# Mixture-of-experts results: scaled at the copy from PSUM and added in memory by the scatter, instead of scattered apart and summed on VectorE

## The reference, cut to what matters

```python
scores = sigmoid(x @ gate_w)                      # 32 experts
...                                               # 2 of 4 groups are masked out, the best 6 of the rest are taken
weights = take_along_axis(original_scores, selected_experts, axis=-1)
weights = weights / sum(weights, axis=-1, keepdims=True)
xs = repeat(x, 6, axis=0)[sort_idx]               # sorted by expert
d = ragged_dot(silu(xs @ w_gate) * (xs @ w_up), w_down, group_sizes)
expert_out = sum(d[unsort_idx].reshape(T, 6, H) * weights[..., None], axis=1)
shared = silu(x @ sw_gate) * (x @ sw_up) @ sw_down
return expert_out + shared
```

## Time and profile before

| | us |
|---|---|
| median of 3 runs | 1883.34 (1881.84 to 1884.39) |
| the profiled execution, its own time | 1883.7 |
| its span | 1881.9 |
| TensorE busy in the span | 1711.4 (91%) |
| VectorE / ScalarE / GpSimd busy | 1413.4 / 1098.0 / 1099.5 |
| `experts`, from its first instruction to its last add | 1296.7 to 1627.6 |

### The profile page before, as it was taken

The page is one execution under the profiler, slowest core; times in us unless marked ns, Lnnn a source line. Parts: engine busy times, 40 slices in busy tenths (PEclk is TensorE's granted clock), DMA queues, the critical chain, the costliest instruction groups (busy, mean ns, idle before and its releaser), DMA issues. The chain is left out here.

```text
span 1881.9 us, 41627 instructions
## 1 busy us (share of the span) xinstructions
PE 1711.4 (91%) x14679; PEld 1308.2 (70%) x14679; DVE 1413.4 (75%) x3752; ACT 1098.0 (58%) x2774; POOL 1099.5 (58%) x1718
## 2 busy tenths in 40 slices
PE   4899999999999999999999999978999997189988
PEld 3678787878777788877877887755555554139974
DVE  7898786888977878878788788766567764775746
ACT  6577776667777667767666676643133332174534
POOL 5578595686776957868668578410366663181210
PEclk9899999999999999999999999997999999596998
DMA  3210111011010000100000000436299895400100
GB/s 124 74 51 30 60 35 53 19 36 46 18 38 31 24 19 18 63 26 19 20 31 23 24 1 24 140 109 227 71 279 269 272 268 173 144 19 23 45 7 26
DMA packets 74649, 140.24 MB, mean 75 GB/s; under 512 B 10921, under 2 KB 44818, under 8 KB 74194
## 3 DMA queue, kind: packets, MB, share of 16 engines
q1 hardware_dynamic: 63634, 105.37, 18.3%
q0 software_dynamic: 9984, 30.42, 4.8%
q10 hardware_dynamic: 832, 1.84, 0.3%
HBM read 111.73 MB, written 25.86 MB: 73 GB/s over the span
## 5 line engine op out<-in xcount | busy, mean ns | idle before, releaser
L920 DVE TENSOR_TENSOR att_pT<-att_pT 128x512 bf16<-128x512 f32 (+1 forms) x512 | 321.1, 651 | 175.6 <-ACT att_pT L729 173.0
L565 PE MATMUL att_out<-att_V,att_pT 128*128 128x128 bf16 x5760 | 388.2, 220 | 13.6 <-DVE att_pT L920 11.8
L565 PEld LDWEIGHTS att_out<-att_V,att_pT 128*128 128x128 bf16 x5760 | 350.3, 98 | 40.5 <-DVE att_pT L920 24.0
L729 ACT ACTIVATE att_pT<-att_pT 128x512 bf16<-128x512 f32 (+1 forms) x512 | 277.9, 571 | 131.9 <-PE att_pT L551 131.9
L735 ACT ACTIVATE att_prob<-att_scores,att_negmax 128x512 f32<-128x512 f32 (+1 forms) x512 | 330.2, 654 | 19.5 <-DVE att_negmax L909 19.5
L542 PE MATMUL att_scores<-att_K,att_Q 128*128 128x512 bf16 (+1 forms) x1536 | 324.9, 361 | 0.1
L907 DVE TENSOR_REDUCE att_mx<-att_scores 128x1 f32<-128x512 f32 (+1 forms) x512 | 291.4, 631 | 1.3 <-PE att_scores L542 1.2
L551 PE MATMUL att_pT<-att_ident,att_prob 128*128 128x128 f32 x1920 | 275.9, 275 | 0.0
L542 PEld LDWEIGHTS att_scores<-att_K,att_Q 128*128 128x128 bf16 x1536 | 151.1, 98 | 145.1 <-issue 3.5
L551 PEld LDWEIGHTS att_pT<-att_ident,att_prob 128*128 128x128 f32 x1920 | 210.1, 141 | 0.9
L465 PE MATMUL att_aux<-att_wkv,att_kvT 128*128 128x256 bf16 x1350 | 168.2, 274 | 22.7 <-DVE att_aT L881 14.8
(11 more groups left out here) (342 smaller groups left out, 3230.2 us busy)
## 6 DMA issues: line engine op xcount, KB each, us to landing
moe_wa<-in_wa_l SPq DMA_DIRECT2D x80, 480.0 KB
att_wq<-wq_s SPq DMA_DIRECT2D x12, 512.0 KB, 3.7
att_wo<-wo_s SPq DMA_DIRECT2D x12, 512.0 KB, 3.8
moe_y<-y_s SPq DMA_DIRECT2D x8, 768.0 KB, 4.5
att_stage<-in_ctx_l SPq DMA_DIRECT2D x9, 512.0 KB, 4.2
near_s<-att_windows POOLq DMA_DIRECT2D x8, 576.0 KB, 5.6
win_near<-near_s SPq DMA_DIRECT2D x32, 144.0 KB
moe_wb<-in_wb_l SPq DMA_DIRECT2D x80, 48.0 KB
```

Source lines behind the costliest of these rows:

```text
L565: last = nc.tensor.matmul(out_ps[:, i % 2, :], pT[:, i % 2, a, k, :], V[:, par, k, w, :], start=(k, a, w) == (0, 0, 0), stop=(k, a) == (KT ...
L729: nc.scalar.activation(pT[:, i % 2, 0, 4 * j:4 * j + m, :], pT_ps[j % 2][:, 0:m, :], ACT.Copy).then_inc(s["pt_hi"], 1)
L920: nc.vector.tensor_tensor(pT[:, i % 2, 1, 4 * j:4 * j + m, :], pT_ps[j % 2][:, 0:m, :], pT[:, i % 2, 0, 4 * j:4 * j + m, :], ALU.subtract) ...
```

## The change

The share no longer meets its row on VectorE behind the scatter, but on ScalarE ahead of it:

- The table `xrow_s` has 32 more columns: each token's gates. SyncE writes them in a DMA at the block's start; the gathers fetch rows of 1152 bytes in place of 1024.
- VectorE makes once a one-hot table of each slot's expert (`tiles_experts`, 128x2560), and for each slot multiplies the gathered gates by it with a running sum (`slot_shares`): one share per lane. ScalarE's copy of the result takes it as its scale.
- The scatter adds to what lies in memory (`compute_op=ALU.add`), into `sum0_s` and `sum1_s` in turn, each with one row per token. A scatter waits until the one two slots before it has landed, as both may hold the same token. GpSimd fills `zeros`, SyncE writes it to both accumulators (1 MB and 128 KB each) ahead of the weight fetches.
- In the end 8 DMAs of 256 KB bring both accumulators back and VectorE adds them with 8 instructions of 128x512. `y6`, `add_row`, `shares` and the turn half of the table are gone.

```diff
+                sp.dma_start(t["xrow_s"][0:TOK, D:XROW].rearrange("(n p) e -> p n e", p=P), gates[:, :, :]).then_inc(s["gates_out"], 16)
                 sp.wait_ge(s["const_in"], 16)
                 sp.dma_start(t["xrow_s"][EMPTY:EMPTY + 1, :], const[0:1, CONST["zero"]]).then_inc(s["zero_out"], 16)
+                sp.wait_ge(s["zeros_set"], 1)
+                for a in range(SUMS):
+                    sp.dma_start(t[f"sum{a}_s"][0:TOK, :].rearrange("(n p) d -> p n d", p=P), zeros[:, :, :]).then_inc(s["sums_zero"], 16)
+                    sp.dma_start(t[f"sum{a}_s"][TOK:TOK + P, :], zeros[:, 0, :]).then_inc(s["sums_zero"], 16)
...
-                for n in range(TT):
-                    wait(sp, s["added"], SHARED + TOPK * (n - 1) if n > 1 else 0)
-                    rows = t["y_s"][0:UNUSED, :].rearrange("(k t) d -> t k d", k=TOPK)
-                    sp.dma_start(y6[:, n % 2, :, :], rows[n * P:(n + 1) * P]).then_inc(back[n % 2], 16)
+                for m in range(TT // 2):
+                    for a in range(SUMS):
+                        rows = t[f"sum{a}_s"][2 * m * P:2 * (m + 1) * P, :].rearrange("(n p) d -> p n d", p=P)
+                        sp.dma_start(sums[:, a, 2 * m:2 * m + 2, :], rows).then_inc(back[m], 16)
...
                 def gather(i):
                     wait(pool, s["xt_done"], i - XRING + 1)
+                    wait(pool, s["share_ready"], i - XRING + 1)
...
                 def scatter(i):
                     pool.wait_ge(s["y_sb"], i + 1)
-                    pool.indirect_dma_start(out=t["y_s"], out_offset=bass.IndirectOffsetOnAxis(ap=result_row[:, i:i + 1], axis=0),
-                                            in_=ysb[:, i % YRING, :], in_offset=None).then_inc(stored[i % YRING], 16)
+                    if i >= SUMS:
+                        pool.wait_ge(stored[(i - SUMS) % YRING], 16 * ((i - SUMS) // YRING + 1))
+                    pool.indirect_dma_start(out=t[f"sum{i % SUMS}_s"], out_offset=bass.IndirectOffsetOnAxis(ap=result_row[:, i:i + 1], axis=0),
+                                            in_=ysb[:, i % YRING, :], in_offset=None, compute_op=ALU.add).then_inc(stored[i % YRING], 16)
...
                 def result(i):
-                    nc.scalar.activation(ysb[:, i % YRING, :], y_ps[i % 2][:, 0:D], ACT.Copy).then_inc(s["y_sb"], 1)
+                    act.wait_ge(s["share_ready"], i + 1)
+                    nc.scalar.activation(ysb[:, i % YRING, :], y_ps[i % 2][:, 0:D], ACT.Copy, scale=share[:, i:i + 1]).then_inc(s["y_sb"], 1)
...
+                def tiles_experts():
+                    V.tensor_tensor(expert_hot[:, :, :], expert_all[:, :].unsqueeze(2).to_broadcast(places), const[:, CONST["lane"]][:, 0:E_ALL].unsqueeze(1).to_broadcast(places),
+                                    ALU.is_equal).then_inc(s["expert_hot"], 1)
+                def slot_shares(i):
+                    dve.wait_ge(s["expert_hot"], 2)
+                    dve.wait_ge(gathered[i % XRING], 16 * (i // XRING + 1))
+                    wait(dve, s["share_ready"], i - 3)
+                    V.scalar_tensor_tensor(hit[:, i % 4, :], xg[:, i % XRING, D:XROW], 1.0, expert_hot[:, i, :], ALU.mult, ALU.mult,
+                                           accum_out=share[:, i:i + 1]).then_inc(s["share_ready"], 1)
...
-                    V.tensor_tensor(tile_hot[:, n % 2, :, 1, :], hit, const[:, CONST["turn"]].unsqueeze(2).to_broadcast(places), ALU.mult)
...
+                    if j == TT + 2:
+                        tiles_experts()
+                    if SHARED <= j < JOBS:
+                        slot_shares(j - SHARED)
```

More of the change, by code:

```diff
@@ L1162 @@
 WRING, XRING, YRING = 8, 12, 4
+SUMS = 2
+XROW = D + E_ALL
 CONST = {}
-for _name, _width in (("tri", P), ("before", E_ALL), ("upto", E_ALL), ("lane", P), ("slot", NSLOT), ("tokm", TT), ("spare", NSLOT), ("turn", TOPK), ("zero", D)):
+for _name, _width in (("tri", P), ("before", E_ALL), ("upto", E_ALL), ("lane", P), ("slot", NSLOT), ("tokm", TT), ("own", 1), ("zero", XROW)):
     CONST[_name] = slice(sum(c.stop - c.start for c in CONST.values()), sum(c.stop - c.start for c in CONST.values()) + _width)
@@ L1381, in experts @@
                  "hot", "table_part", "table_ready", "rows_ready",
-                 "xt_done", "xt_sb", "up_done", "silu_done", "h_done", "ht_done", "ht_sb", "y_done", "y_sb", "added", "quant", "share_step"]
+                 "xt_done", "xt_sb", "up_done", "silu_done", "h_done", "ht_done", "ht_sb", "y_done", "y_sb", "added", "quant",
+                 "zeros_set", "sums_zero", "gates_out", "expert_hot", "share_ready"]
         s = {n: sc.sem(n) for n in names}
-        load, stored, gathered, back = ([sc.sem(f"{n}{i}") for i in range(r)] for n, r in (("load", WRING), ("stored", YRING), ("gathered", XRING), ("back", 2)))
+        load, stored, gathered, back = ([sc.sem(f"{n}{i}") for i in range(r)] for n, r in (("load", WRING), ("stored", YRING), ("gathered", XRING), ("back", TT // 2)))
         route(nc, t, x, h32, sel, selb, gates, wabs, wvo, [
@@ L1448, in _ @@
                 pool.wait_ge(s["rows_ready"], 1)
+                pool.wait_ge(s["sums_zero"], 32 * SUMS)
                 for i in range(NSLOT):
@@ L1472, in experts_of_tiles @@
                     pe.wait_ge(s["begun_ready"], 1)
-                    nc.tensor.matmul(expert_ps, ones[0:E_ALL, 0:E_ALL], begun[:, :], start=True, stop=True).then_inc(s["expert_done"], 1)
+                    nc.tensor.matmul(expert_ps, ones[0:E_ALL, :], begun[:, :], start=True, stop=True).then_inc(s["expert_done"], 1)
                 def table(n):
@@ L1479, in table @@
                     for k in range(TOPK):
-                        last = nc.tensor.matmul(token_ps, lane_hot[:, n % 2, k, :], tile_hot[:, n % 2, k, :, :], start=(n, k) == (0, 0), stop=(n, k) == (TT - 1, TOPK - 1))
+                        last = nc.tensor.matmul(token_ps, lane_hot[:, n % 2, k, :], tile_hot[:, n % 2, k, :], start=(n, k) == (0, 0), stop=(n, k) == (TT - 1, TOPK - 1))
                     last.then_inc(s["table_part"], 1)
@@ L1609, in token_table @@
                     dve.wait_ge(s["table_part"], TT)
[L1610 to L1616, removed]
+                    V.tensor_scalar(token_row[:, :], token_ps, float(EMPTY), None, ALU.add).then_inc(s["table_ready"], 1)
+                    link(V.tensor_scalar(spare[:, :], token_ps, 0.0, const[:, CONST["own"]], ALU.is_ge, ALU.mult))
+                    V.scalar_tensor_tensor(result_row[:, :], token_ps, float(EMPTY), spare[:, :], ALU.add, ALU.add).then_inc(s["rows_ready"], 1)
                 def hidden(j):
@@ L1633, in add_shared @@
                     V.tensor_tensor(x[:, j // 2, :], x[:, j // 2, :], y_ps[j % 2][:, 0:D], ALU.add).then_inc(s["added"], 1)
[L1635 to L1644, removed]
                 def quantize(n):
@@ L1665, in quantize, with add_sums @@
                     then(V.tensor_tensor(wq_flat[:, part], y8[:, :], over[:, :], ALU.subtract), QUANT_STEPS)
[L1667 to L1671, removed]
-                    V.scalar_tensor_tensor(x[:, n, :], y6[:, n % 2, k, :], share[:, n, k:k + 1], x[:, n, :], ALU.mult, ALU.add).then_inc(s["added"], 1)
+                def add_sums(m, a):
+                    if a == 0:
+                        dve.wait_ge(back[m], 16 * SUMS)
+                    two = slice(2 * m, 2 * m + 2)
+                    dve.wait_ge(s["added"], SHARED + (TT // 2) * a if a else SHARED)
+                    V.tensor_tensor(x[:, two, :], x[:, two, :], sums[:, a, two, :], ALU.add).then_inc(s["added"], 1)
                 tiles_and_slots()
@@ L1696, in _ @@
                 assert part == PARTS
-                dve.wait_ge(s["share_step"], 3 * TOPK)
-                for q in range(TT * TOPK):
-                    add_row(q)
+                for a in range(SUMS):
+                    for m in range(TT // 2):
+                        add_sums(m, a)
 def window_attention(nc, t, x, hhl, wabs, wvo):
@@ L2106, in program @@
     scratch("mean_s", [B, ROW], F32)
-    scratch("xrow_s", [TOK + 1, D], F32)
-    scratch("y_s", [UNUSED + NSLOT * P, D], F32)
+    scratch("xrow_s", [TOK + 1, XROW], F32)
+    for a in range(SUMS):
+        scratch(f"sum{a}_s", [TOK + P, D], F32)
     scratch("near_s", [TOK * WIN, ROW], F32)
@@ L2167, in layout @@
     table[:, CONST["slot"]] = np.arange(NSLOT)
-    table[:, CONST["turn"]] = np.arange(TOPK) - TOPK
-    table[:, CONST["spare"]] = np.arange(P)[:, None] + P * np.arange(NSLOT)
+    table[:, CONST["own"]] = np.arange(P)[:, None]
     table[:, CONST["tokm"]] = np.arange(P)[:, None] + P * np.arange(TT) - EMPTY
```

27 lines of the change are left out of this document (15 added, 12 removed).

## The result

| | before | after |
|---|---|---|
| median, us | 1883.34 (1881.84 to 1885.90, 7 runs) | 1889.82 (1886.96 to 1892.24, 7 runs) |
| ratio, 95% interval | | 1.0031 (1.0021 to 1.0040) |
| profiled execution, us | 1883.7 | 1888.1 |
| span | 1881.9 | 1886.3 |

The account below looks back on a forecast made before the run. Slots were taken to go at TensorE's pace, then 34.2 us of summing on the path. Terms -21.9 + 1.0 + 7.0 - 3.2 + 1.4 = -15.7 took 1883.7 to 1868; forecast's own range 1859 to 1877, whole range 1860 to 1912.

Parts of the forecast that it names:

- The scatter's wait: GpSimd's wait for the landing two slots back: about 5.2 us, inside two slots' 6.18, so 0; 8.3 would cost 84 us.
- Rival B: GpSimd's issue becomes the bound: a scatter's issue grows from 0.99 past 1.50 us; at 1.98, +38 us, 1906; chance 0.12.
- A: Rival: the chain of scatters waiting for landings becomes the bound; each us above 6.18 costs 40; at 7.0, 1901; chance 0.22.
- C: Rival: the DMA engines become the bound, 0.13 us short in 72 slots that fetch weights; +9 us, 1877; chance 0.13.
- The sum: Adding up behind the experts: 2.10 MB read back instead of 6.3, 12.3 us in place of 34.2, -21.9 us.
- The last scatter: From the last scatter's issue to SyncE moving on, 2.46 us before: the adding scatter's extra read costs +1.0 us.
- The tables: Table jobs: `hot` loses a 0.65 us instruction in each of 8 jobs; -3.2 us, between 0 and -5.2.
- the one-hot table: VectorE's one-hot table of experts, 2560 columns, 2.85 us, partly in idle time: +1.4 us once (0 to 2.9).
- The share per slot: VectorE's 80 multiplies, 0.22 us each, counting only ahead of 32 quantize chains: +7.0 us, bounds 2.6 and 17.6.
- At nothing: Zero and gate writes, GpSimd's fill, ScalarE's scaled copy and the gather's share wait: no cost; uncovered, the writes and fill 8 us.

Follow-up runs that it names:

- sums3_yring8: The changed kernel with three accumulators in turn (a scatter waits for the one three before) and 8 result buffers instead of 4: 1876.04 us, ratio 0.9950.
- few_weights: The changed kernel without the weight fetches of slots 8 to 79, which compute with the weights of the first eight: 1873.05 us (one execution).
- plain: The changed kernel with its adding scatter made a plain write again, same waits and same two memory tables: 1865.68 us, ratio 0.9906.
- xring20_sums3_yring8: The changed kernel with 20 gather buffers instead of 12, three accumulators and 8 result buffers instead of 4: 1871.86 us, ratio 0.9935.

## Why the prediction was wrong, by its steps

- *The scatter's wait*, "I take **0**", failed. In its place the runs showed 18.8 us of waits for landings in the changed kernel, and 0.3 with a third accumulator (`sums3_yring8`). It had the right place, and a fair middle for the landing: 5.2 estimated, 5.7 measured. Two things were wrong. It set the landing alone against the two slots, but the next scatter starts 0.77 us after the landing; its 2.46 us of the plain scatter end with SyncE's next DMA, which in the changed kernel follows the landing by 0.1 us, and the gathers' 4.5 end with the landing. So what had to stay under 6.18 was 5.7 + 0.77 = 6.4, and it did not. And it set one number against the threshold: the landings run from 3.6 to 7.6, and a short one gives nothing to a long one, because nothing behind the wait has slack to catch up. The bound from above, 8.3, was near the longest that any run showed, 8.2.
- *Rival B* named its mechanism rightly, and B came true beside A: the issue rose to 1.59, just past the 1.50 that were free. Its price does not hold. By it, 0.09 over the threshold in 80 slots would be 7 us. `few_weights` has 13.0 us up to the last gather, where a slot of `plain` takes 3.01 us and not the 3.09 assumed, then 5.5 back behind it, as there is no gather in the last 11 slots. The sum, 7.5, is close to 7 by luck, and 4.0 of it are waits for landings.
- The prediction gave A and B a chance each and none to both at once, which is what happened: 257.7 us of scatters against 234.5 in `plain`. Of these 23.2, 18.8 are the waits; the other 4.4 are GpSimd's own longer pace.
- *C*: the estimate of an adding scatter's extra load, 0.45 us of all engines, is met: with three accumulators the share rose from 0.88 to 1.01, 0.13 x 140 us / 44 scatters = 0.41. The rule quoted there (the Trainium skill, Collectives: The Full Stack, section The bandwidth ceiling: two reads for an add) fits that; the 1.93 given with it is the page's ratio of the rates of two collectives. The bound it was to make did not come, at a share of 1.01 in `sums3_yring8`.
- The fixed cost quoted under A (the Trainium skill, DMA: Bandwidth & Descriptors, section Anatomy of one DMA), by which this transfer would land in an estimated 2.3 us, is not met by the adding scatter: its shortest landing of any run is 3.5 us, and with the weight fetches gone (share 0.55) the median is 3.8.
- *The sum*: 12.3 forecast, 12.4 measured. *The last scatter*: +1.0 forecast, +1.2 measured (whether its reads overlap, as the forecast supposed, no run shows). *The tables* and *the one-hot table*: together -1.8 forecast, -1.9 measured. That is closer than such a reading can be: counted from the block's first instruction on GpSimd, the first result copy starts 62.6 us later in the kernel before and 60.0 to 60.9 in the changed kernel and its variants, which is -1.7 to -2.6.
- *The share per slot*: +7.0 forecast, 4.4 to 4.9 measured, inside its bounds. One takes 0.19 us with its accumulator read, not 0.22. That alone gives 6.1; that some of the 32 chains had room for it would explain the rest, but no run shows it.
- *At nothing*: the zeros went earlier than supposed, ahead of the weight fetches (share 0.72 from 1296 to 1305, 0.03 before), and pushed SyncE's first fetch from 1303.90 to 1305.42. No engine waits for a weight fetch in the trace from 1340 to 1610. From 1320 to 1330 the share is 0.12. ScalarE's copy with a scale became 0.09 us longer (0.47 against 0.38); what that costs is inside the 4.4 of the shares.
- Missed entirely: when GpSimd falls behind, its arrears stand at the end too, 3.4 us more between the last copy and the last scatter.

## What to carry to other kernels

A wait on a transfer is to be held against the slack with the longest landing that the load gives, not with the median, unless something behind the wait can catch up. To the landing comes the time until the waiting engine starts, here 0.77 us. And the slack is to be computed with the new price of every instruction on that engine, all changes together. One more buffer in such a chain is the cheap test and the cheap cure: here the third accumulator was worth 13 us and the fourth minus 3. Look for the late engine by following the waits round: TensorE was seen to wait for VectorE, and the cause lay three steps further: ScalarE, GpSimd, the landing.

## What the runs showed of the hardware

**An indirect scatter that adds costs GpSimd 0.6 us more to issue.** 1.59 us against 0.99, at a DMA share of 0.97 and of 0.55 (`few_weights`). The page's queue table has, first of the changed kernel, then of `plain`, which differs in nothing but the adding:

```profile
q0 software_dynamic: 17664, 31.73, 8.0%
```

```profile
q0 software_dynamic: 9984, 31.73, 5.4%
```

The same bytes, 7680 packets more: 96 per scatter.

**Two of GpSimd's indirect DMAs never follow closer than 0.30 us**, so the gather costs 1.29 and the adding scatter 1.89. The shortest gap in any run is 0.303.

**A scatter that waits for a landing starts late.** From the landing of one adding scatter to the start of the one that waited for it are 0.77 us while gathers run beside them, 0.73 among the last ten scatters. ScalarE's copies start 0.07 us after the landing that they waited for.

**A fill on GpSimd and a cast on VectorE stopped each other.** In the changed kernel:

```profile
1296.56 2.02 DVE L1592 CAST moe_cast<-moe_const 128x192 bf16<-128x192 f32 x1 [0.97 <-PEq L75]
...
1296.66 1.80 POOL L1440 MEMSET moe_zeros<- 128x2048 f32 x1
```

The cast took 0.28 us before. It ends 0.12 us after the fill does, and the first `moe_tile_hot` of the tables starts 1.0 us later after the block's start. The same happened in `plain` and `xring20_sums3_yring8`. In the other eight runs with the fill the cast took 0.28 us, and the fill 1.92 in place of 1.80. The cast's record starts 0.10 us ahead of the fill's in all of them, so that order does not tell which one is stopped. The Trainium skill, SBUF — State Buffer, section Who interferes with whom, says that the two engines share a port pair, which a cast can take in a two-port mode, that the one which issues first holds it for a whole instruction, and that the other waits. The traces agree as to the hold; of the order of issue they show only the records, and those don't decide. The first result copy shows little of it: 60.5 to 60.9 us after the block's start in the three runs, 60.0 to 60.7 in the eight. Moving the fill was not tried.

What stays open: why an adding scatter's landing spreads from 3.5 to 8.2 us under load. The load is part of it (at a share of 0.55 it is 3.6 to 4.2), but which transfers it stands behind no run told.
